# The attention part's per-batch chain spread over four slots, and the last batch routed as one group: cross-attention and a sparse two-expert network on one core

## What is computed

```python
def _L0_xattn_ref(p, k_v, W_k, b_k, ln_gamma, ln_beta):
    kv = k_v @ W_k.T + b_k
    out = jnp.einsum('bij,bjd->bid', p, kv)
    sim = jnp.einsum('bid,bjd->bij', out, kv) * scale
    ...
    sim = (sim - mu) * jax.lax.rsqrt(var + EPS) * ln_gamma + ln_beta
    return jax.nn.softmax(sim, axis=-1)

def _L0_ffn_ref(x, Wg, W1, W2, W3):
    scores = jnp.einsum('btd,ed->bte', x, Wg)
    topk_s, topk_i = jax.lax.top_k(scores, TOP_K)
    probs = jax.nn.softmax(topk_s, axis=-1)
    ...
    for e in range(E):
        h = jax.nn.silu(jnp.einsum('btd,hd->bth', x, W1[e])) * jnp.einsum('btd,hd->bth', x, W2[e])
        y = y + w[..., e:e + 1] * jnp.einsum('bth,dh->btd', h, W3[e])
    return y
x = x + _L0_xattn_ref(_layernorm(x, axis=-1), ctx_512, ...)
x = x + _L0_ffn_ref(_layernorm(x, axis=-1), ...)
```

## Time and profile before

| | |
|---|---|
| Median of 3 runs | 407.45 us (405.23 to 407.67) |
| Profiled execution | 405.16 us |
| Its span, first to last instruction | 403.3 us |
| Attention part and drain, to the first gather | 131.31 us |
| Mean granted clock of PE | 0.938 |
| Busy in the span: PE, DVE, ACT, POOL | 89%, 68%, 66%, 40% |

### The profile page before, as it was taken

How to read it: one execution, slowest core, us unless ns; L and a number is a source line. 1 busy time by engine, 2 the same in 40 slices (tenths; PEclk the granted TensorE clock), 3 DMA queues, 4 the chain that set the end, 5 groups by cost and what they waited for, 6 DMA issues and landing times.

```text
span 403.3 us, 8243 instructions
## 1 busy us (share of the span) xinstructions
PE 359.9 (89%) x2301; PEld 237.5 (59%) x2301; DVE 272.8 (68%) x709; ACT 265.2 (66%) x457; POOL 160.6 (40%) x189
## 2 busy tenths in 40 slices
PE   6876988989787678899999999999999999999981
PEld 5553656756585444555666666666666666666650
DVE  1253574979968889999667676676766767667660
ACT  1277686778866697897656666566665666656650
POOL 2124453454740503464543424435244352443422
PEclk9999989899855599999999999999999999999997
DMA  7998789986950212235435354353453645535333
GB/s 231 420 413 336 259 275 339 399 280 228 277 183 2 79 28 54 54 55 101 82 81 105 60 101 79 79 103 67 96 81 80 103 62 98 81 80 101 67 45 52
DMA packets 21834, 57.61 MB, mean 143 GB/s; under 512 B 4832, under 2 KB 4960, under 8 KB 20256
## 3 DMA queue, kind: packets, MB, share of 16 engines
q0 software_dynamic: 8736, 20.53, 28.4%
...
q10 hardware_dynamic: 2016, 14.94, 10.3%
...
## 4 chain that ended last, share of the span: by engine, by line
PE 56%; DVE 9%; issue 4%; ACT 3%; DMA 2%; POOL 1%; POOLq 0%; ACTq 0%; DVEq 0%
PE bank L1208 32%; PE bank L1242 16%; PE bank L1199 4%; PE bank L1228 3%; DVE Wp L794 2%; DMA out<-kvj_s,sidx 1%; DVE stage L941 1%; ACT stage L620 1%; DMA ng_s<-n_table,gidx 1%; PE bank L1116 1%; DVE x_s L973 1%; DVE kvg_s L947 1%; PE bank L1100 1%; PE bank L1043 0%; DVE stage L820 0%
## 5 line engine op out<-in xcount | busy, mean ns | idle before, releaser
L941 DVE SCALAR_TENSOR_TENSOR stage<-W,w3sc,stage 128x512 f16<-128x512 f16 x117 | 84.1, 747 | 7.5 <-ACT stage L620 7.5
L1242 PE MATMUL bank<-stage,n_s 128*128 128x512 f16 (+1 forms) x351 | 82.2, 379 | 2.8 <-issue 1.5
L1208 PE MATMUL bank<-Wp,kvg_s 128*128 x480 | 79.9, 317 | 4.6 <-DVE kvg_s L947 4.6
L620 ACT ACTIVATE stage<-W,w3sc 128x512 f16 x117 | 80.1, 717 | 0.0
L1208 PE MATMUL bank<-Wp,kv_s 128*128 x456 | 74.3, 313 | 3.2 <-DVE kv_s L947 3.2
L1208 PEld LDWEIGHTS bank<-Wp,kvg_s 128*128 128x128 f16 x480 | 47.3, 99 | 31.5 <-issue 6.1
L469 POOL DMA_INDIRECT out<-oT_s,sidx x20 | 34.2, 1708 | 75.8 <-ACT oT_s L647 65.0
L1208 PEld LDWEIGHTS bank<-Wp,kv_s 128*128 128x128 f16 x456 | 44.4, 98 | 28.1 <-issue 4.5
L965 DVE TENSOR_TENSOR n_s<-bank,n_s 128x384 f16<-128x384 f32 x39 | 21.7, 556 | 55.1 <-ACT n_s L633 55.1
L469 POOL DMA_INDIRECT out<-kvj_s,sidx x19 | 32.5, 1711 | 66.1 <-ACT kvj_s L647 63.6
L1242 PEld LDWEIGHTS bank<-stage,n_s 128*128 128x128 f16 (+1 forms) x351 | 34.2, 98 | 36.1 <-issue 3.3
...
## 6 DMA issues: line engine op xcount, KB each, us to landing
...
Wp<-in_w SPq DMA_DIRECT2D x2, 1408.0 KB, 12.7
...
```

The source lines that it names most:

```text
L620: eng.activation(w3p[t % 2][:, c * D:(c + 1) * D], W3[:, bass.ds(e * W3N + c * D, D)], ACT.Copy, scale=w3sc[:, bass.ds(e, 1)]).then_inc(s_ ...
L941: eng.scalar_tensor_tensor(w3p[r][:, W3N + c * D:W3N + (c + 1) * D], W3[:, bass.ds(e * W3N + c * D, D)], w3sc[:, bass.ds(e, 1)], w3p[r][:, ...
L1208: mm = eng.matmul(bank[2 * which + r][:, 0:H], n_, w_, start=(c == 0 and k == 0), stop=(c == DC - 1 and k == 2))
L1242: mm = eng.matmul(ybank(t - 1)[:, :], h_, w_, start=(c == 0 and k == 0), stop=(c == HC - 1 and k == 2))
```

## The change

- **Chain of a batch**: gram and outs go to the end of slot 0 on PE; o_evac to slot 1 and kvj_evac ahead of the sum of squares on ACT; gram_outs to the start and squares to the end of slot 2 on PE; keys to the start of slot 3; square_in to slot 2 on DVE; mean_square between x_stats and scale_in in slot 3. On DVE the row min comes first in every slot, ahead of x_stats. sims are in one place in all slots, behind the router. SP loads the next xT in slot 1.
- **Router**: one group for each batch, so `GROUPS` is gone; class sums are those of the batch alone, and rank adds up all earlier ones. places and columns go to slots 12 to 18, the last behind the slots.
- **Router weights**: dlt, wden, the reciprocal (now a power of -1) and the product go from DVE to POOL: dlt in slot 0 ahead of the norm, the others in slot 1 behind gamma_keys. `top` has two batches of room.
- **Warming**: 20 matmuls in place of 12 while the first gather runs, and 10 new ones in slot 17. low_rows(1) goes ahead of w3_low in the first expert tile.

```diff
-GROUPS = ((0, 4), (4, 4), (8, 4), (12, 3), (15, 1))
-WARM_GATHER = 12
+WARM_GATHER = 20
+WARM_DRAIN = 10
@@ SP slot
-                if i == TPB - 1 and real(b + 2) and b >= -1:
+                nxt = 1 if b < 0 else b + 2
+                if (b < 0 or i == 1) and real(nxt):
@@ POOL
+            def router_gap(b):
+                cols = bass.ds(b * TPB, TPB)
+                eng.wait_ge(s_ti, TPB * (b + 1) + 1)
+                pair = slice(b % 2 * TPB, (b % 2 + 1) * TPB)
+                eng.tensor_tensor(dlt[:, cols], top[:, pair, 1], top[:, pair, 0], ALU.subtract).then_inc(s_dl, 1)
+            def router_weights(b):
...
+                eng.tensor_tensor(wden[:, cols], edl[:, cols], ones[:, 0:TPB], ALU.add).then_inc(s_wd, 1)
...
+                eng.tensor_tensor(w1, wden[:, cols], mone[:, 0:1].to_broadcast([P, TPB]), ALU.pow).then_inc(s_w1, 1)
...
+                eng.tensor_tensor(w2, edl[:, cols], w1, ALU.mult).then_inc(s_w2, 1)
@@ POOL slot
+                if i == 0 and real(b - 2):
+                    router_gap(b - 2)
                 b1, i1 = lag(b, i, 1)
                 if real(b1):
                     norm(b1, i1)
                 if i == 1 and real(b + 1):
                     gamma_keys(b + 1)
+                if i == 1 and real(b - 2):
+                    router_weights(b - 2)
@@ ACT slot, behind scaled
-                if i == 2 and real(b + 1):
+                if i == 0 and real(b + 1):
+                    kvj_evac(b + 1)
+                if i == 1 and real(b + 1):
                     o_evac(b + 1)
...
-                if i == 0 and real(b + 1):
-                    kvj_evac(b + 1)
@@ DVE slot
-                if i == 3 and real(b + 1):
-                    square_in(b + 1)
-                bn_, in_ = lead(b, i)
-                if real(bn_):
-                    x_stats(bn_, in_)
-                    if i < TPB - 1:
-                        scale_in(bn_, in_)
                 if real(b):
...
+                bn_, in_ = lead(b, i)
+                if real(bn_):
+                    x_stats(bn_, in_)
+                    if i == 3:
+                        mean_square(b + 1)
+                    scale_in(bn_, in_)
                 b1, i1 = lag(b, i, 1)
...
                 if i == 2 and real(b + 1):
+                    square_in(b + 1)
+                if i == 1 and real(b + 1):
                     gram_copy(b + 1)
...
-                if n == 20:
-                    places(3)
-                    columns(3)
+                if n == 18:
+                    columns(2)
...
-                if n in (11, 14, 18):
-                    columns((n - 11) // 3 if n < 18 else 2)
+                if n in (12, 14, 17):
+                    places((n - 12) // 2)
+                if n in (13, 15):
+                    columns((n - 13) // 2)
@@ PE drain
                 if n == 17:
                     router(B - 1, 0)
+                    rank(2)
+                    warm(ones16[:, :], WARM_DRAIN)
                     turn_n(B - 1, 2)
                     router(B - 1, 1)
```

More of the change, by code:

```diff
@@ L892, in then @@
                 eng.wait_ge(s_r, steps[0])
-            last = len(GROUPS) - 1
-            router_weights(B - 1)
-            places(last)
-            columns(last)
+            places(B - 1)
+            columns(B - 1)
             eng.wait_ge(s_cntp, 1)
```

145 lines of the change are left out of this document (60 added, 85 removed).

## The result

The kernel after takes 416.95 us as a median of 4 runs (415.93 to 418.28), the kernel before 407.56 beside it on the same chip: ratio 1.0238, 95% interval 1.0179 to 1.0298. Run again on another chip it took 416.36 against 406.73, ratio 1.0243 (1.0201 to 1.0284). It is slower by 2.4%; 408.0 was predicted, with a range up to 413.0.

What follows compares the result with a forecast made beforehand. It took TensorE as busy 89% of the span, with the change in the first 131 us, where TensorE, VectorE and ScalarE are near their limit. Terms -0.4+2.0+0.25-1.3 = +0.55 gave a median of 408.0 us, range 400.5 to 413.

Steps and rivals of the forecast that it cites:

- Batches 0 to 2: Chain from keys to kvg, timed from K, the start of kvj_evac(b+1): -0.4 us, bounds -1.9 and +1.0.
- the fall: TensorE's clock may drop between turn_n and the sims waiting for kvg: up to 1.3 in batch 0, 1.6 in batch 1.
- the -2.7: Batch 0: with no router yet and kvj_evac earlier, K comes at 49.85 in place of 52.55.
- Router weights in batch 2: router_weights(0) between gamma_keys and alpha(2,3) on GpSimd takes 1.7; the exponential of batch 3 comes at K+20.95, +1.15.
- the 0.4 on top: GpSimd and VectorE lock each other out, so each batch's three weight steps would end some 0.4 later; total +0.95.
- Batch 3: VectorE gains columns(0), loses small router steps and starts nearer to ScalarE: +2.0 us, bounds +1.0 and +2.75.
- Drain: Last x1 to first gather: -1.65 ahead of the scores of tile 15, +1.9 behind; sum +0.25, bounds -1 and +1.
- Gather and first tiles: Longer warming gives full clock from the first transposes, low_rows(1) fills a VectorE wait: -1.3 us, bounds 0 and -1.8.
- The third: Rival: the clock's fall hits outs in slot 0, +2.4 in each of three batches, median 415.2 us; chance 0.18.
- The first: Rival: the drain runs at full clock, scores of tile 15 3.4 us earlier, median 404.6 us; chance 0.18.
- The second: Rival: the spread chain takes the waits out, a batch goes down to 20 us, median 400.9 us; chance 0.22.

Runs made afterwards that it cites:

- a_warm: The kernel after with 24 more warming matmuls in slot 2, ahead of the sims that wait for kvg: 412.28 us.
- a_gk: The kernel after with gamma_keys(b+1) ahead of the norm of tile (b,0) on GpSimd in slot 1: 409.15 us.
- b_rw: The kernel before with the router's difference and weights on GpSimd, the exponential at the end of slot 0: 412.15 us.
- c_cols0: c_best with rank, places, columns and table of batch 0 back in their slots of before: 401.84 us.
- a_grp: The kernel after with the last batch routed in two groups, tiles 12 to 14 and then tile 15: 413.66 us.
- a_drain: The kernel after with the drain's TensorE order of before, without warming matmuls ahead of the transposes of tile 14: 414.68 us.
- a_wdve: The kernel after with router difference and weights back on VectorE and the exponential in its old place: 413.93 us.
- c_best_w12: c_best with 12 warming matmuls in place of 20 during the gather, and low_rows(1) behind w3_low(0) again: 401.45 us.
- c_best: The kernel after with gamma_keys ahead of norm, sims(b,3) ahead of gram, weights on VectorE, last batch in two groups, old drain order: 401.78 us.

## Why the prediction was wrong

1. **Batches 0 to 2, forecast -0.4, measured +7.1 in the one profile and +5.3 in the other. This is the step that failed.** Its places were right: o_evac at K+6.95 after a wait of 2.5 (K+7.07, 2.38; the terms given for it, K+5.1, 0.9 and 1.1, add to K+7.1 and not to K+6.9), gamma_keys at K+10.3 to K+11.5 (K+10.75), scaled(b,3) at K+12.1 (K+12.6). Wrong was the sentence after them, "From there ScalarE's own work carries on", with 11.4 left to the next K. With the clock held up, in a_warm, it is 12.0 from scaled(1,3) to the next K, 0.6 more than I gave; in after it is 13.3 with TensorE at half clock. I had listed the sims that wait for kvg with squares, keys and routers behind them and didn't price TensorE's idle time there as the one that brings the clock down; the fall stood in the sum at half of its bound. In batch 0, where K was to come 2.7 earlier, at 49.85, it came at 54.93; in a_gk it came at 49.87. So the -2.7 was there to be had, and the late kvg took it. In batch 2 the late kvg cost 1.2 to 1.6 with the clock up, and this was in no term either.
2. **The weighing that failed with it.** I compared o_evac with o_evac, K+6.95 against K+10.1, and called it earlier. The sims need kvg as well, and the moment when the last of both is there went from K+10.7 (o_evac's end) to K+12.0 (gamma_keys' end). A chain is timed by the last input.
3. **Router weights in batch 2, forecast +1.15.** From K to the exponential K+20.95 was forecast; a_gk has 20.89 and b_rw 21.14 (before 19.78), so this size was right. b_rw has 1.25 more in batch 3, where I had counted only VectorE's relief of 0.8 and forgot alpha(3,3). In batch 2 of after the three steps ran from 93.16 to 94.75, 1.6 where 1.7 was taken, so the 0.4 on top, for steps locked out by VectorE, was not there. The clock on top, in most executions, was in no term. Alone in the kernel before, this edit costs 5.8.
4. **Batch 3, forecast +2.0, measured +2.3**: right, and c_cols0 shows the cause by taking it away. In that stretch, that is: the time didn't fall with it.
5. **Drain, forecast +0.25, measured +3.4.** Behind the scores +1.9 was forecast and +2.2 measured, which a_grp takes back. (The 8.1 worked out for it took 8.75; it was held against 6.2 where the rows have 6.54, so its own numbers give +1.6.) Ahead of them -1.65 was forecast and +1.2 measured. The step was that rank(2) and the warming go "into its wait for the norm": TensorE comes to that place with table(0) and a router step still to do at half clock, has no wait left there, and the transposes of tile 14 start at 5.2 and not at 2.0 behind the last x1. a_drain shows it, with 2.0 back. The router weights on GpSimd add to it through the norm of tile 13: a_wdve has 1.2 back in the same stretch. This was in no term.
6. **Gather and first tiles, forecast -1.3, measured -0.4 and -0.85 in the two profiles of after.** Over all profiles it is -1.2, so the term was about right, though the runs of c_best_w12 don't show it. In the first profile of after the first up still ran at half clock (3.49). The idle time ahead of it, 1.46, isn't the cause: c_best idles the same 1.46 there and runs it at full clock (1.96). Why the clock falls there in one and not in the other is open.
7. **The rivals.** The third, slower through the clock, gave 415.2 and came close to 416.95, by another way than it said: outs ran at full speed in batches 1 and 2 (3.60; 4.85 in batch 0 in the first profile, 3.60 in the second), and the clock fell one step later, at the sims. The first (the drain at full clock) is refuted, 0.50 throughout. The second, a spread chain without waits, is the better half of the truth: with gamma_keys ahead of the norm and sims(b,3) ahead of gram the chain does get to 22.96 from K to K, though not to its 20.
